# Slot table of the expert routing: one-hot blocks in bf16, built by VectorE alone

## The reference, cut to what matters

```python
logits = jnp.einsum('bsh,eh->bse', x, router_w) + expert_bias
scores = jax.nn.softmax(logits, axis=-1)
top_w, top_idx = jax.lax.top_k(scores, TOP_K)          # 4 of 16 experts
top_w = top_w / jnp.sum(top_w, axis=-1, keepdims=True)
...
sel = jnp.take_along_axis(out, top_idx[..., None], axis=2)
return jnp.sum(sel * top_w[..., None], axis=2)
```

## Time and profile before

| | |
|---|---|
| Median of 3 runs | 1520.33 us (1519.51 to 1523.01) |
| Profiled execution | 1521.97 us |
| Span of its instructions | 1519.4 us |
| Busy: TensorE, VectorE, ScalarE, GpSimd | 1295.9, 966.3, 653.8, 821.3 us |
| Mean granted TensorE clock | 0.947 |
| Linear attention and before | to about 102 us |
| Routing (VectorE L678 to L798) | 102.4 to 172.3 us |
| of it the 64 slot matmuls, L782 to L788 | 127.4 to 170.8 us |
| First gather of the experts | 174.2 us |

### The profile page before, as it was taken

How to read it: one execution, slowest core, us unless ns; L and a number is a source line. 1 busy time by engine, 2 the same in 40 slices (tenths; PEclk the granted TensorE clock), 3 DMA queues, 4 the chain that set the end, 5 groups by cost and what they waited for, 6 DMA issues and landing times. The chain is left out here.

```text
span 1519.4 us, 23881 instructions
## 1 busy us (share of the span) xinstructions
PE 1295.9 (85%) x7096; PEld 976.6 (64%) x7097; DVE 966.3 (64%) x2055; ACT 653.8 (43%) x1183; POOL 821.3 (54%) x652
## 2 busy tenths in 40 slices
PE   6965799999944899998999987799999999888797
PEld 5854455555523677776776767677676777767675
DVE  4568422222217778877687768768777877875555
ACT  3211233333212555555555553265555555555332
POOL 2016688888845455545455556354555555556444
PEclk9976799999985999999999999999999999999899
DMA  9357255555552000000000000000000000002001
GB/s 326 121 167 175 86 83 80 80 82 80 80 107 67 8 8 8 1 7 7 1 7 0 2 0 12 15 1 8 8 7 0 7 7 0 1 1 62 1 14 42
DMA packets 66218, 67.13 MB, mean 44 GB/s; under 512 B 15040, under 2 KB 59648, under 8 KB 66016
## 3 DMA queue, kind: packets, MB, share of 16 engines
q1 hardware_dynamic: 48048, 42.38, 9.5%
q0 software_dynamic: 15168, 20.72, 8.8%
q10 hardware_dynamic: 2928, 3.15, 0.7%
HBM read 45.12 MB, written 21.10 MB: 44 GB/s over the span
## 5 line engine op out<-in xcount | busy, mean ns | idle before, releaser
L1525 POOL TENSOR_TENSOR att_prob_lo<-att_prob,att_prob_hi 128x896 fp32r<-128x896 f32 (+1 forms) x192 | 380.4, 1981 | 223.4 <-ACT att_prob_hi L1472 223.4
L1386 PE MATMUL all_bank<-att_q_hl,sequence_k_hl 128*128 128x512 f32 (+2 forms) x1152 | 289.4, 361 | 43.2 <-DVE att_minus L1593 43.0
L1578 DVE TENSOR_REDUCE att_peak<-all_bank 128x1 f32<-128x512 f32 (+3 forms) x384 | 207.8, 550 | 95.0 <-PE all_bank L1373 61.2
L1406 PE MATMUL all_bank<-att_prob_hi,sequence_v_hl 128*128 128x512 f32 (+2 forms) x768 | 225.1, 376 | 12.1 <-ACT late_oT L1481 12.1
L1386 PEld LDWEIGHTS all_bank<-att_q_hl,sequence_k_hl 128*128 128x128 f32 x1152 | 191.6, 192 | 63.9 <-DVE att_minus L1593 33.3
L1465 ACT ACTIVATE att_prob<-all_bank 128x896 f32<-128x896 f32 (+1 forms) x192 | 162.8, 848 | 157.8 <-PE all_bank L1392 156.4
L1370 PE MATMUL all_bank<-sequence_k_hl,att_q_hl 128*128 128x512 f32 (+3 forms) x384 | 164.7, 432 | 6.8 <-DVE att_peak L1578 6.8
L1472 ACT CAST att_prob_hi<-att_prob 128x896 fp32r<-128x896 f32 (+1 forms) x192 | 168.4, 877 | 2.6
L1519 POOL TENSOR_TENSOR att_rows<-att_by_cos,att_by_sin 128x128 f32<-128x128 f32 x128 | 58.5, 457 | 198.6 <-DVE att_by_sin L1564 198.6
L903 PE MATMUL all_bank<-early_w_gu,moe_xgT 128*128 x316 | 147.2, 548 | 3.6 <-issue 2.4
L1406 PEld LDWEIGHTS all_bank<-att_prob_hi,sequence_v_hl 128*128 128x128 f32 x768 | 128.5, 191 | 27.0 <-issue 16.6
(11 more groups left out here) (244 smaller groups left out, 2299.7 us busy)
## 6 DMA issues: line engine op xcount, KB each, us to landing
sequence_w_raw<-wqk_rows SPq DMA_DIRECT2D x16, 256.0 KB, 2.7
early_w_gu<-in_gate SPq DMA_DIRECT2D x16, 224.0 KB, 5.4
early_w_gu<-in_up SPq DMA_DIRECT2D x16, 224.0 KB, 5.5
early_w_down<-in_down SPq DMA_DIRECT2D x1, 3584.0 KB, 20.5
sums<-early_zero SPq DMA_DIRECT2D x18, 128.0 KB, 3.6
all_xT<-in_xT SPq DMA_DIRECT2D x4, 512.0 KB, 8.7
all_x_tok<-in_x SPq DMA_DIRECT2D x1, 2048.0 KB, 17.1
x_rows<-all_x_tok SPq DMA_DIRECT2D x4, 512.0 KB, 3.0
```

What stands on the lines that cost most here:

```text
L1386: nc.tensor.matmul(ps, k_hl[:, ks, j * P:(j + 1) * P], q_hl[r // 2 % 2][:, qs, r % 2, q0:q0 + w], start=n == 0, stop=False)
L1406: mm = nc.tensor.matmul(pv_ps[:, q0 - qc * WIDE:WIDE], v_hl[:, vs, j, :], part[:, x % 3, a:z], start=j == 0 and n == 0, stop=last and n == 2)
L1525: nc.gpsimd.tensor_tensor(prob_lo[:, x % 3, a:z], prob[:, x % 2, a:z], prob_hi[:, x % 3, a:z].bitcast(F32), ALU.subtract).then_inc(lo_sb, 1)
L1578: nc.vector.tensor_reduce(peak[:, r % 2, n, i:i + 1], max_ps[y % 2][:, 0:w], AX_X, ALU.max).then_inc(peak_sb, 1)
```

## The change

- `is_lo` and `is_hi` become bf16 and are rings of six (HOTS). A bf16 copy of the column numbers, `iota_bf`, is made for the comparisons.
- bf16 holds integers exactly to 256 only, and 8 bits of a weight. So `is_hi` has five parts (PARTS) instead of three: the high and the low digit of the token number plus one, and three parts of the weight, each the rounding of what the ones before leave. The moving operand has 430 columns instead of 258.
- VectorE makes all of both: for each of the 64 groups one comparison for `is_lo`, and one instruction per part for `is_hi`. GpSimd's comparisons, its cast of the token numbers, and the semaphores `place_sb`, `lo_sb` and `lo4_sb` go. TensorE waits for `hot_sb` alone.
- GpSimd's eight subtractions of the values stay, one behind the other.
- Reading the table puts the digits and the three weight parts together.

```diff
+    HOTS = 6
+    TOKEN, WEIGHT, PARTS = 0, 2, 5
...
-        is_lo = m.sb("is_lo", [P, 2, TOPK, P], F32R)
-
-        is_hi = m.sb("is_hi", [P, 4, 3, WIDTH_HOT], F32R)
-        held = m.sb("held", [P, 3, NT, TOPK])
-        weight_hi = m.sb("weight_hi", [P, NT, TOPK], F32R)
-        token1 = m.sb("token1", [P, NT])
+        is_lo = m.sb("is_lo", [P, HOTS, P], BF16)
+
+        is_hi = m.sb("is_hi", [P, HOTS, PARTS, WIDTH_HOT], BF16)
+        iota_bf = m.sb("iota_bf", [P, P], BF16)
+        held = m.sb("held", [P, PARTS, NT, TOPK])
+        weight_hi = m.sb("weight_hi", [P, 2, NT, TOPK], BF16)
+        token1_parts = m.sb("token1_parts", [P, 2, NT], I32)
...
                 for n in range(NT * TOPK):
-                    t, k = divmod(n, TOPK)
-                    if t % 4 == 3:
-                        pe.wait_ge(lo4_sb, t // 4 + 1)
-                    else:
-                        pe.wait_ge(lo_sb, n + 1 - t // 4 * TOPK)
                     pe.wait_ge(hot_sb, n + 1)
-                    nc.tensor.matmul(slot_ps, is_lo[:, t % 2, k, :], is_hi[:, n % 4].rearrange("p a s -> p (a s)"),
+                    nc.tensor.matmul(slot_ps, is_lo[:, n % HOTS, :], is_hi[:, n % HOTS].rearrange("p a s -> p (a s)"),
                                      start=n == 0, stop=n == NT * TOPK - 1).then_inc(slot_mm, 1)
...
-                for t in range(NT):
-                    if t % 2 == 0 and t >= 4:
-                        values_low(t // 2 - 2)
-                    if t % 4 == 3:
-                        continue
-                    if t >= 2:
-                        pool.wait_ge(slot_mm, (t - 1) * TOPK)
-                    for k in range(TOPK):
-                        n = t * TOPK + k
-                        nc.gpsimd.tensor_scalar(is_lo[:, t % 2, k, :], cst["iota"], lo[:, n:n + 1], None,
-                                                ALU.is_equal).then_inc(lo_sb, 1)
-                for n in range(PAIRS - 2, PAIRS):
+                for n in range(PAIRS):
                     values_low(n)
...
-                dve.wait_ge(spread_sb, 2)
-                step.up(v.tensor_copy(held[:, 0], token1[:].unsqueeze(2).to_broadcast([P, NT, TOPK])))
-                step.up(v.tensor_copy(weight_hi[:], held[:, 1]))
-                step.settle()
-                step.up(v.tensor_tensor(held[:, 2], held[:, 1], weight_hi[:].bitcast(F32), ALU.subtract))
+                dve.wait_ge(spread_sb, 1)
+                step.up(v.tensor_scalar(token1_parts[:, 0], token1_i[:], 7, None, ALU.arith_shift_right))
+                step.up(v.tensor_scalar(token1_parts[:, 1], token1_i[:], P - 1, None, ALU.bitwise_and))
+                step.up(v.tensor_copy(weight_hi[:, 0], held[:, WEIGHT]))
+                step.up(v.tensor_copy(iota_bf[:], cst["iota"]))
+                step.settle()
+                for i in range(2):
+                    step.up(v.tensor_copy(held[:, TOKEN + i], token1_parts[:, i].unsqueeze(2).to_broadcast([P, NT, TOPK])))
+                step.up(v.tensor_tensor(held[:, WEIGHT + 1], held[:, WEIGHT], weight_hi[:, 0], ALU.subtract))
+                step.settle()
+                step.up(v.tensor_copy(weight_hi[:, 1], held[:, WEIGHT + 1]))
+                step.settle()
+                step.up(v.tensor_tensor(held[:, WEIGHT + 2], held[:, WEIGHT + 1], weight_hi[:, 1], ALU.subtract))
                 step.settle()
                 for n in range(NT * TOPK):
                     t, k = divmod(n, TOPK)
-                    if t % 4 == 3 and k == 0:
-                        dve.wait_ge(slot_mm, (t - 1) * TOPK)
-                        v.tensor_tensor(is_lo[:, t % 2], cst["iota"].unsqueeze(1).to_broadcast([P, TOPK, P]),
-                                        lo[:, n:n + TOPK].unsqueeze(2).to_broadcast([P, TOPK, P]),
-                                        ALU.is_equal).then_inc(lo4_sb, 1)
-                    if n >= 4:
-                        dve.wait_ge(slot_mm, n - 3)
-                    v.scalar_tensor_tensor(is_hi[:, n % 4],
-                                           cst["iota"][:, 0:WIDTH_HOT].unsqueeze(1).to_broadcast([P, 3, WIDTH_HOT]),
-                                           hi[:, n:n + 1], held[:, :, t, k].unsqueeze(2).to_broadcast([P, 3, WIDTH_HOT]),
-                                           ALU.is_equal, ALU.mult).then_inc(hot_sb, 1)
+                    if n >= HOTS:
+                        dve.wait_ge(slot_mm, n - HOTS + 1)
+                    v.tensor_scalar(is_lo[:, n % HOTS, :], iota_bf[:], lo[:, n:n + 1], None, ALU.is_equal)
+                    for i in range(PARTS):
+                        ins = v.tensor_scalar(is_hi[:, n % HOTS, i, :], iota_bf[:, 0:WIDTH_HOT], hi[:, n:n + 1],
+                                              held[:, i, t, k:k + 1], ALU.is_equal, ALU.mult)
+                    ins.then_inc(hot_sb, 1)
                 dve.wait_ge(slot_mm, NT * TOPK)
-                slots = slot_ps.rearrange("p (a s) -> p a s", a=3)[:, :, 0:ST]
-                step.up(v.tensor_copy(slot_w_hi[:], slots[:, 1]))
-                step.settle()
-                step.up(v.tensor_tensor(slot_w[:], slots[:, 2], slot_w_hi[:], ALU.add))
-                step.up(v.tensor_scalar(slot_f[:], slots[:, 0], -1.0, None, ALU.add))
-                step.up(v.tensor_scalar(empty[:], slots[:, 0], 0.5, None, ALU.is_lt))
+                slots = slot_ps.rearrange("p (a s) -> p a s", a=PARTS)[:, :, 0:ST]
+                step.up(v.tensor_copy(slot_w_hi[:], slots[:, WEIGHT]))
+                step.up(v.tensor_scalar(slot_high[:], slots[:, TOKEN], float(P), -1.0, ALU.mult, ALU.add))
+                step.settle()
+                step.up(v.tensor_tensor(slot_w_mid[:], slots[:, WEIGHT + 1], slot_w_hi[:], ALU.add))
+                step.up(v.tensor_tensor(slot_f[:], slots[:, TOKEN + 1], slot_high[:], ALU.add))
+                step.settle()
+                step.up(v.tensor_tensor(slot_w[:], slots[:, WEIGHT + 2], slot_w_mid[:], ALU.add))
+                step.up(v.tensor_scalar(empty[:], slot_f[:], -0.5, None, ALU.is_lt))
```

More of the change, by code:

```diff
@@ L528, in phase_route @@
         slot_f = m.sb("slot_f", [P, ST])
+        slot_high = m.sb("slot_high", [P, ST])
         slot_w_hi = m.sb("slot_w_hi", [P, ST])
+        slot_w_mid = m.sb("slot_w_mid", [P, ST])
         spare = m.sb("spare", [P, ST])
@@ L544, in phase_route @@
         a_mm, a_sb, vo_mm, vo_sb, vo_lo_sb = (m.sem(n) for n in ("a_mm", "a_sb", "vo_mm", "vo_sb", "vo_lo_sb"))
-        place_sb, dve_sb, count_mm, hot_sb, lo_sb, slot_mm = (
-            m.sem(n) for n in ("place_sb", "dve_sb", "count_mm", "hot_sb", "lo_sb", "slot_mm"))
-        expo_sb, shifted_sb, chosen_sb, spread_sb, lo4_sb = (
-            m.sem(n) for n in ("expo_sb", "shifted_sb", "chosen_sb", "spread_sb", "lo4_sb"))
+        dve_sb, count_mm, hot_sb, slot_mm = (m.sem(n) for n in ("dve_sb", "count_mm", "hot_sb", "slot_mm"))
+        expo_sb, shifted_sb, chosen_sb, spread_sb = (
+            m.sem(n) for n in ("expo_sb", "shifted_sb", "chosen_sb", "spread_sb"))
         rank_ps = bank[:, 1, 0:N]
         tally_ps = bank[:, 2, 0:N]
-        slot_ps = bank[:, 3, 0:3 * WIDTH_HOT]
+        slot_ps = bank[:, 3, 0:PARTS * WIDTH_HOT]
         by_e = lambda a: a.rearrange("p (t e) -> p t e", e=E)
@@ L650, in _ @@
                 token.up(nc.gpsimd.iota(token1_i[:], pattern=[[P, NT]], base=1, channel_multiplier=1))
-                token.settle()
-                token.up(nc.gpsimd.tensor_copy(token1[:], token1_i[:]))
-                pool.wait_ge(place_sb, 1)
                 def values_low(n):
@@ L746, in _ @@
                 step.settle()
-                v.tensor_copy(lo[:], lo_i[:].rearrange("p t k -> p (t k)")).then_inc(place_sb, 1)
+                step.up(v.tensor_copy(lo[:], lo_i[:].rearrange("p t k -> p (t k)")))
                 step.up(v.tensor_copy(hi[:], hi_i[:].rearrange("p t k -> p (t k)")))
@@ L756, in _ @@
                     for k in (k0, k0 + 1):
-                        step.up(v.tensor_reduce(held[:, 1, :, k], match_w[:, k - k0], AX_X, ALU.add))
+                        step.up(v.tensor_reduce(held[:, WEIGHT, :, k], match_w[:, k - k0], AX_X, ALU.add))
                     step.settle()
```

## The result

| | before | after |
|---|---|---|
| Median | 1520.56 us (4 runs, 1519.51 to 1523.01) | 1562.9 us (4 runs, 1555.86 to 1568.23) |
| Ratio | | 1.0272, 95% interval 1.0242 to 1.0302 |
| Profiled execution | 1521.97 us, clock 0.947 | 1561.2 us, clock 0.926 |
| From VectorE's first one-hot block to the reading of the table | 43.4 us | 82.4 us |

The change makes the kernel 2.7% slower, 42 us by the medians; the forecast was 1561 us. The profiled execution is 39.2 us longer.

A forecast was written before the change was run, and what follows sets the result against it. The routing stage was taken as a coupled loop with GpSimd mostly last; with VectorE making all blocks it grows from 43.4 to 84.0 us, with step 5 +41.0 us, giving 1561 us, range 1551 to 1574.

The forecast's parts named there:

- Step 1: Slot loop on VectorE: six instructions take 1.22 us a slot, 78.3 us for 64, 9.2 us either way for streaming.
- Step 2: In the stage, seven GpSimd subtractions stretch VectorE's instructions by 0.59 us each, 4.1 us in all.
- 3: set-up, from L768 or L753: Ahead of the first slot, the set-up takes 1.5 us, 0.9 more than before.
- 4: last comparison to reading: End of the stage, from VectorE's last comparison to L788 reading the table: 0.7 us.
- 5: after the table: Behind the table, the weight needs two additions in sequence, one more settled step: 0.4 us more.
- step 6: TensorE's slot matmuls and foldings take 43 us beside 84 us of VectorE: no cost, with 2 us in the range.
- rival E: A small VectorE instruction costs 0.06 us fixed, as the smallest row shows: stage 37.9 us, end 1515 us; chance 0.03.
- B: In VectorE's slot instructions bf16 streams no faster than the casts: 9.2 us more, 1570 us; chance 0.22.
- C: VectorE's slot instructions stream at 1.04 ns an element: 28 us more, 1589 us; chance 0.09.
- D: Fetching scalars overlaps VectorE's instruction ahead, leaving 0.07 us fixed: stage 41.7 us, end 1519 us, no change; chance 0.04.
- Behind the table: The phases behind the table are shifted, not changed; a change of more than 2 us would refute the forecast.

The follow-up runs named there:

- experiment 5: Changed kernel without GpSimd's eight subtractions, the low parts zeroed once: stage 79.2 us against 82.4, whole time 1566.8 us (1 run).
- experiment 8: Kernel before, with VectorE making half of the row blocks in large instructions: stage 38.1 us against 43.4, ratio 0.9993; run again 40.4 us, 1.0001.
- experiment 1: Changed kernel with 72 extra VectorE instructions of seven kinds ahead of the slot loop: stage 82.2 us without them, whole time 1578.7 us (1 run).
- experiment 10: Changed kernel with two copies of each slot matmul into an unread PSUM bank: stage 83.3 us against 82.4, whole time 1566.7 us (1 run).
- experiment 6: Changed kernel with four parts instead of five, the weight's third part left out: stage 69.7 us against 82.4, whole time 1545.7 us (1 run).
- experiment 3: Kernel before (fp32r, three parts), all blocks made by VectorE in small instructions, rings of six: stage 62.4 us, whole time 1532.4 us (1 run).
- experiment 4: Changed kernel with the 64 row blocks made by GpSimd: stage 78.2 us against 82.4, whole time 1556.1 us (1 run).
- experiment 7: Changed kernel with rings of four instead of six: stage 82.1 us against 82.4, whole time 1559.0 us (1 run).

## Why the prediction was right

The forecast was 1561 us, the median 1562.9; the difference that counts is that of the profiles, since it can be followed by steps.

| step | forecast, us | measured, us |
|---|---|---|
| 1: one slot | 1.22 | 1.23 (0.161 + 5 × 0.213) |
| 1: 64 slots | 78.3 | 78.5 |
| 2: GpSimd's subtractions | 4.1 (0 to 5.1) | 3.1 (experiment 5) |
| 3: set-up, from L768 or L753 | 1.5, 0.9 more | 1.45, 0.9 more |
| 4: last comparison to reading | 0.7 | 0.7 |
| 5: after the table | 0.4 more | 0.4 more |
| sum | 41.0 | 40.2 |
| profiled execution | 41.0 more | 39.2 more |

Of the 1.0 us between the last two rows, 0.2 comes from a setting-up that began earlier (126.57 instead of 126.80 us), and 0.8 lies outside the span of the instructions (1521.97 − 1519.4 before, 1561.2 − 1559.4 after).

- **What bounds.** Before, a loop of three engines with GpSimd mostly last: experiment 8 shows it, since relieving GpSimd shortened the stage. One figure was read wrongly. I added TensorE's groups to 43.1 us of a 43.4 us stage; the window gives 35.2 us busy, since overlapping durations were counted twice. It bore on step 6 and on rival E, where it made TensorE look nearer to being the bound than it was.
- **Step 1** carried the prediction, and rested on prices of long instructions (256 and 258 elements) applied to 86. They hold to a hundredth of a microsecond. So does the streaming rate, 0.27 ns an element in experiment 1. But it had been taken as the middle of two bounds, 9.2 us to either side, with no row behind the choice; as far as the rows go, that it came out so well is luck.
- **Step 2** was a third too high. It took 0.59 us from one place, with an instruction of two inputs on VectorE; on the small ones a subtraction costs 0.44.
- **Steps 3 to 5** hold within 0.1 us.
- **Step 6** held: no cost, although the clock stayed at 0.50 for the whole stage. TensorE's busy time was 56.5 of 82.4 us at that clock, and at 0.88 the stage was no shorter (experiment 10).
- **The rivals.** B and C fell by the spacing of 0.213 us. D fell: scalars cost 0.06 us each in instructions of 86 and of 16 elements alike; their fetch is not hidden behind the instruction ahead. E fell with it.
- **Behind the table** I expected no change, with 2 us as the bound, and the sum agrees (1347.0 and 1347.1 us). That it agrees so well is luck. In the thirteen profiles, whose programs are the same behind the table's chain, this stretch takes from 1345.8 to 1356.5 us. In the two compared here, the experts' phase became 2.5 us longer and the last output block of the attention 2.7 shorter (from its first matmul to the first of the feed-forward block: 38.6 and 36.0 us; in the other profiles 35.9 to 38.7, with no pattern by kernel). The mechanism is shown by the steps up to the table; that the whole time came within 2 us of the forecast owes something to chance, as four executions of the changed kernel lie 12 us apart.

## What to carry to other kernels

Price a plan of many small VectorE instructions by the spacing of starts, not by elements: here 0.07 us fixed, plus 0.06 for each per-partition scalar read from memory, and the elements on top. A faster data type that splits one instruction into five lost here, even at four times the streaming rate; one broadcast instruction at a quarter of that rate was 30 us better over 64 groups. And when an engine takes over work that ran beside it, ask first whether it can take it in large pieces: the same move in pieces of 512 and 258 elements cost nothing.

## What the runs showed of the hardware that I had not expected

- The price adds up: a scalar from memory costs 0.061 us in instructions of 16 and of 86 elements, in bf16 and in f32 (experiment 1), and L464 with 256 f32 elements fits with 0.06.
- How much GpSimd holds VectorE up is not the length of GpSimd's instruction. A subtraction of 0.77 us cost VectorE 0.44 over an instruction of 86 elements and up to 0.57 over one of 128 (experiment 6); a comparison of 0.60 us cost about 0.1.
- Whole times scatter with the granted clock. For the changed kernel the four runs were 1555.9, 1561.2, 1564.6 and 1568.2 us at mean clocks of 0.929, 0.926, 0.925 and 0.924. The profiles show two places of the scatter. One is behind the table, as said above. The other is ahead of the routing: in experiments 3, 4, 6 and 7 the stage starts at 118.9 to 120.1 us, in the others at 125.3 to 128.5 (with the price list of experiment 1, the list does). In these others TensorE sits idle for 4.8 to 5.8 us before its third run of L241, and in the four it does not. First the changed kernel, then experiment 7:

```profile
31.89 8.14 PE L241 MATMUL all_bank<-lin_w_hl,lin_x_hl 128*128 128x512 f32 x24 [4.83 <-issue]
25.93 5.68 PE L241 MATMUL all_bank<-lin_w_hl,lin_x_hl 128*128 128x512 f32 x24
```

Why it does so is not known. The profiles of the kernel before and of the changed kernel both have this pause, so it doesn't bear on their difference. In this kernel a gain of 5 us in one stage is plain in a trace and lost in the medians of 12 runs.
